# Cross attention in a decoder layer: two chunks of heads pass each stage of the loop together

## What is computed

```python
# per batch (8): L = 256 tokens, D = 128, H = 16 heads of DH = 64
q = layernorm(x) @ Wq          # 256 x 1024
k, v = layernorm(ctx) @ Wkv    # 256 x 1024 each
p = softmax(q k^T * DH**-0.5)  # per head, 256 x 256
x = layernorm(x + (p v) @ Wo + bo)
```

## Time and profile before

| | us |
|---|---|
| median of 3 runs (lowest, highest) | 2374.88 (2374.52, 2377.05) |
| span of the profiled execution | 2376.2 |
| PE busy over the span | 2232.7 (94%) |
| DVE busy | 1862.1 (78%) |
| ACT busy | 1703.2 (72%) |
| POOL busy | 1649.6 (69%) |
| mean granted TensorE clock | 0.981 |

### The profile page before, as it was taken

The page is one execution under the profiler, slowest core; times in us unless marked ns, Lnnn a source line. Parts: engine busy times, 40 slices in busy tenths (PEclk is TensorE's granted clock), DMA queues, the critical chain, the costliest instruction groups (busy, mean ns, idle before and its releaser), DMA issues. The chain is left out here.

```text
span 2376.2 us, 69401 instructions
## 1 busy us (share of the span) xinstructions
PE 2232.7 (94%) x26001; PEld 1464.0 (62%) x26001; DVE 1862.1 (78%) x2680; ACT 1703.2 (72%) x3299; POOL 1649.6 (69%) x1553
## 2 busy tenths in 40 slices
PE   5889779999799999999999999999999999999996
PEld 3555446666456666666666666666666666666664
DVE  4899957777678888888888888888888888887884
ACT  5889734544377787787787777787777777777774
POOL 4777832323478778778787787787787787787782
PEclk8999989999899999999999999999999999999997
DMA  2312210000022222222222222222222222222221
GB/s 76 111 59 68 69 51 2 1 1 1 20 63 67 56 76 66 61 71 66 64 68 66 68 65 66 72 61 67 74 58 67 78 54 67 78 53 67 78 53 52
DMA packets 103196, 140.36 MB, mean 59 GB/s; under 512 B 63072, under 2 KB 64096, under 8 KB 102752
## 3 DMA queue, kind: packets, MB, share of 16 engines
q1 hardware_dynamic: 103136, 139.57, 21.7%
HBM read 56.39 MB, written 1.31 MB: 24 GB/s over the span
## 5 line engine op out<-in xcount | busy, mean ns | idle before, releaser
L1799 PE MATMUL f_psA<-f_W,f_xT 128*128 (+1 forms) x1152 | 602.0, 632 | 20.7 <-DVE f_m L1607 12.5
L1607 DVE TENSOR_TENSOR f_m<-f_psA,f_tab 128x1024 f32<-128x1024 f32 x384 | 461.5, 1222 | 120.2 <-ACT f_sq L1468 106.1
L1357 POOL TENSOR_TENSOR f_Pr<-f_Pr,f_rden 128x384 f32<-128x384 f32 x384 | 311.5, 832 | 236.6 <-DVE f_rden L1586 236.6
L1385 POOL TENSOR_TENSOR f_qkr<-f_qkr,f_rn 128x1024 f32<-128x1024 f32 x192 | 361.5, 1904 | 0.2 <-POOL f_rn L1393 0.2
L1799 PEld LDWEIGHTS f_psA<-f_W,f_xT 128*128 128x128 f32 x1152 | 188.9, 190 | 164.5 <-issue 113.4
L1468 ACT ACTIVATE f_sq<-f_psA 128x512 f32<-128x512 f32 x384 | 228.2, 594 | 78.8 <-PE f_psA L1799 76.0
L1770 PEld LDWEIGHTS f_psO<-f_PT,f_V 96*64 96x64 f32 x6144 | 203.5, 138 | 96.4 <-issue 88.5
L1375 POOL TENSOR_TENSOR f_qkr<-f_m 128x512 f32<-128x512 f32 x192 | 244.2, 1272 | 9.1 <-DVE f_m L1607 9.1
L1376 POOL TENSOR_TENSOR f_qkr<-f_m 128x512 f32<-128x512 f32 x192 | 244.2, 1272 | 0.0
L1770 PE MATMUL f_psO<-f_PT,f_V 96*64 96x64 f32 x6144 | 231.9, 227 | 1.6 <-ACT f_PT L1443 1.5
L794 POOL TENSOR_TENSOR x_Es<-x_E 128x512 f32<-128x512 f32 x64 | 81.1, 1267 | 206.1 <-DVE x_E L899 206.1
(11 more groups left out here) (167 smaller groups left out, 4873.5 us busy)
## 6 DMA issues: line engine op xcount, KB each, us to landing
f_V<-f_Vt SPq DMA_DIRECT2D x96, 384.0 KB, 4.2
f_V<-f_Vt SPq DMA_DIRECT2D x96, 256.0 KB, 3.5
f_W<-in_f_W SPq DMA_DIRECT2D x48, 344.0 KB, 3.2
m_Cb<-m_BC_rows SPq DMA_DIRECT2D x64, 256.0 KB, 3.2
f_W<-in_f_W SPq DMA_DIRECT2D x48, 296.5 KB, 4.2
f_V<-f_Vt SPq DMA_DIRECT2D x48, 128.0 KB, 5.3
f_xsA<-xall SPq DMA_DIRECT2D x97, 32.0 KB
f_xsA<-xall SPq DMA_DIRECT2D x97, 31.8 KB
```

What stands on the lines that cost most here:

```text
L1357: pool.tensor_tensor(pv, pv, rv.unsqueeze(3).broadcast_to([P, 2, 2, KEYS]), ALU.mult).then_inc(Pr_ready[g][j], 1)
L1385: pool.tensor_tensor(qv, qv, rv.unsqueeze(3).broadcast_to([P, 2, GH, DH]), ALU.mult).then_inc(qkr_ready[g], 1)
L1607: dve.tensor_tensor(m12[:, j, :, half].rearrange("p m (h d) -> p m h d", d=DH), psA[n % 2][:, :].rearrange("p (h d) -> p h d", d=DH).unsqu ...
L1799: pe.matmul(psA[n % 2][:, :], xT[:, t, :], weights(i, W_QKV + n * 512, 512), start=True, stop=True).then_inc(A_full[n_fill], 1)
```

## The change

The loops go over pairs of chunks (g = 0, 2, 4, ...). Each engine's queue has both chunks of a pair at every stage. The whole output projection of the batch before is done in the pair c = 2, and so are its residual and moments. E has four buffers instead of two (ES = 4). In `scores` the key tile is the outer loop and the head the inner one, and there is one wait for both heads.

```diff
--- before.py
+++ after.py
@@ -691,6 +691,7 @@
     R = 2 * TPB
     LOADS = 16 * 7
     CHUNKS = B * NC
+    ES = 4
     LO, HI = float(np.exp(-11.0)), float(np.exp(11.0))
 
     with ExitStack() as ctx:
@@ -713,7 +714,7 @@
         ctxT = sb("x_ctxT", [P, 2, L])
         V1 = sb("x_V1", [P, 2, TPB, H, DH])
         qk = sb("x_qk", [P, 2, 2, L])
-        E = sb("x_E", [P, 2, 2, TPB, L])
+        E = sb("x_E", [P, ES, 2, TPB, L])
         Es = sb("x_Es", [P, 2, 2, L])
         rden = sb("x_rden", [P, 2, L])
         OT = sb("x_OT", [P, 2, NC, L])
@@ -747,19 +748,19 @@
 
         block = ctx.enter_context(nc.Block())
 
-        fills = [(0, "cat"), (0, "qk0")]
-        for g in range(CHUNKS + 1):
+        fills = [(0, "cat"), (0, "qk0"), (0, "qk1")]
+        for g in range(0, CHUNKS + 1, 2):
             b, c = divmod(g, NC)
-            if g + 1 < CHUNKS:
-                fills.append(((g + 1) // NC, f"qk{(g + 1) % NC}"))
             if g == 0:
                 fills += [(0, f"v{n}") for n in range(4)]
-            if c == 1 and b >= 1:
+            if c == 2 and b >= 1:
                 fills.append((b - 1, "wo"))
-            if c == 3 and b + 1 < B:
+            if g + 2 < CHUNKS:
+                fills += [((g + 2) // NC, f"qk{(g + 2) % NC}"), ((g + 3) // NC, f"qk{(g + 3) % NC}")]
+            if c == 2 and b + 1 < B:
                 fills.append((b + 1, "cat"))
             if c >= 4 and b + 1 < B:
-                fills.append((b + 1, f"v{c - 4}"))
+                fills += [(b + 1, f"v{c - 4}"), (b + 1, f"v{c - 3}")]
         fills.append((B - 1, "wo"))
         place = {f: (k % 2, k // 2) for k, f in enumerate(fills)}
 
@@ -791,7 +792,7 @@
                 if g >= 2:
 
                     pool.wait_ge(O_full, g - 1)
-                pool.tensor_tensor(Es[:, g % 2, :, :], E[:, g % 2, :, 0, :], E[:, g % 2, :, 1, :], ALU.add).then_inc(Es_ready, 1)
+                pool.tensor_tensor(Es[:, g % 2, :, :], E[:, g % ES, :, 0, :], E[:, g % ES, :, 1, :], ALU.add).then_inc(Es_ready, 1)
 
             def add_bias(b):
                 if b >= 1:
@@ -839,10 +840,10 @@
             def exponentials(g):
                 for j in range(2):
                     act.wait_ge(S_full, 2 * g + j + 1)
-                    if j == 0 and g >= 2:
-
-                        act.wait_ge(O_full, g - 1)
-                    act.activation(E[:, g % 2, j, :, :], psS[(2 * g + j) % 4][:, :, :], ACT.Exp, scale=DH ** -0.5).then_inc(E_exp, 1)
+                    if j == 0 and g >= ES:
+
+                        act.wait_ge(O_full, g - ES + 1)
+                    act.activation(E[:, g % ES, j, :, :], psS[(2 * g + j) % 4][:, :, :], ACT.Exp, scale=DH ** -0.5).then_inc(E_exp, 1)
 
             def copy_qk(g):
                 ps, free = wait_fill(act, g // NC, f"qk{g % NC}")
@@ -854,23 +855,27 @@
             deviation(0)
             scale_transposed(0)
             copy_qk(0)
-            for g in range(CHUNKS + 1):
+            copy_qk(1)
+            for g in range(0, CHUNKS + 1, 2):
                 b, c = divmod(g, NC)
-                if g + 1 < CHUNKS:
-                    copy_qk(g + 1)
                 if g < CHUNKS:
                     exponentials(g)
+                    exponentials(g + 1)
                 if g == 0:
                     for n in range(4):
                         evacuate_v(0, n)
-                if c == 1 and b + 1 < B:
+                if g + 2 < CHUNKS:
+                    copy_qk(g + 2)
+                    copy_qk(g + 3)
+                if c == 0 and b + 1 < B:
                     deviation(b + 1)
-                if c == 3 and b >= 1:
+                if c == 4 and b >= 1:
                     deviation2(b - 1)
-                if c == 3 and b + 1 < B:
+                if c == 2 and b + 1 < B:
                     scale_transposed(b + 1)
                 if c >= 4 and b + 1 < B:
                     evacuate_v(b + 1, c - 4)
+                    evacuate_v(b + 1, c - 3)
             deviation2(B - 1)
 
         @block.vector
@@ -896,7 +901,7 @@
             def clip(g):
                 for j in range(2):
                     dve.wait_ge(E_exp, 2 * g + j + 1)
-                    dve.tensor_scalar(E[:, g % 2, j, :, :], E[:, g % 2, j, :, :], LO, HI, ALU.max, ALU.min).then_inc(E_ready, 1)
+                    dve.tensor_scalar(E[:, g % ES, j, :, :], E[:, g % ES, j, :, :], LO, HI, ALU.max, ALU.min).then_inc(E_ready, 1)
 
             def normalise(g):
                 dve.wait_ge(O_full, g + 1)
@@ -920,21 +925,24 @@
 
             statistics(0)
             hats(0)
-            for g in range(CHUNKS + 1):
+            for g in range(0, CHUNKS + 1, 2):
                 b, c = divmod(g, NC)
-                if c == 2 and b >= 1:
-                    residual(b - 1)
                 if g < CHUNKS:
                     clip(g)
-                if g >= 1:
+                if c == 2 and b + 1 < B:
+                    hats(b + 1)
+                if g >= 2:
+                    normalise(g - 2)
+                if g < CHUNKS:
+                    clip(g + 1)
+                if g >= 2:
                     normalise(g - 1)
                 if c == 0 and b + 1 < B:
                     statistics(b + 1)
-                if c == 2 and b + 1 < B:
-                    hats(b + 1)
                 if c == 2 and b >= 1:
+                    residual(b - 1)
                     moments2(b - 1)
-                if c == 4 and b >= 1:
+                if c == 6 and b >= 1:
                     finish(b - 1)
             residual(B - 1)
             moments2(B - 1)
@@ -974,14 +982,14 @@
 
             def scores(g):
                 wait_evacuated(pe, g // NC, f"qk{g % NC}")
-                for j in range(2):
-                    h = 2 * g + j
-                    if h >= 4:
-                        pe.wait_ge(E_exp, h - 3)
-                    r = slice(j * DH, (j + 1) * DH)
-                    for kt in range(TPB):
-                        ins = pe.matmul(psS[h % 4][:, kt, :], qk[r, g % 2, 1, kt * P:(kt + 1) * P], qk[r, g % 2, 0, :], start=True, stop=True)
-                    ins.then_inc(S_full, 1)
+                if g >= 2:
+                    pe.wait_ge(E_exp, 2 * g - 2)
+                for kt in range(TPB):
+                    for j in range(2):
+                        r = slice(j * DH, (j + 1) * DH)
+                        ins = pe.matmul(psS[(2 * g + j) % 4][:, kt, :], qk[r, g % 2, 1, kt * P:(kt + 1) * P], qk[r, g % 2, 0, :], start=True, stop=True)
+                        if kt == TPB - 1:
+                            ins.then_inc(S_full, 1)
 
             def times_v(g):
                 b, c = divmod(g, NC)
@@ -994,7 +1002,7 @@
                     pe.wait_ge(O_free, g - 1)
                 for kt in range(TPB):
                     for j in range(2):
-                        pe.matmul(psO[g % 2][j * DH:(j + 1) * DH, 0, :], V1[:, b % 2, kt, 2 * c + j, :], E[:, g % 2, j, kt, :],
+                        pe.matmul(psO[g % 2][j * DH:(j + 1) * DH, 0, :], V1[:, b % 2, kt, 2 * c + j, :], E[:, g % ES, j, kt, :],
                                   start=(kt == 0), stop=(kt == TPB - 1), skip_group_check=True)
                 pe.wait_ge(Es_ready, g + 2)
                 for j in range(2):
@@ -1015,25 +1023,29 @@
 
             transpose_rows(0)
             project(0)
-            for g in range(CHUNKS + 1):
+            project(1)
+            for g in range(0, CHUNKS + 1, 2):
                 b, c = divmod(g, NC)
-                if g + 1 < CHUNKS:
-                    project(g + 1)
-                if c == 2 and b >= 1:
-                    out_projection(b - 1, 1)
                 if g < CHUNKS:
                     scores(g)
+                    scores(g + 1)
                 if g == 0:
                     for n in range(4):
                         project_v(0, n)
-                if g >= 1:
+                if g >= 2:
+                    times_v(g - 2)
                     times_v(g - 1)
-                if c == 1 and b >= 1:
+                if c == 2 and b >= 1:
                     out_projection(b - 1, 0)
-                if c == 3 and b + 1 < B:
+                    out_projection(b - 1, 1)
+                if g + 2 < CHUNKS:
+                    project(g + 2)
+                    project(g + 3)
+                if c == 2 and b + 1 < B:
                     transpose_rows(b + 1)
                 if c >= 4 and b + 1 < B:
                     project_v(b + 1, c - 4)
+                    project_v(b + 1, c - 3)
             out_projection(B - 1, 0)
             out_projection(B - 1, 1)
```

## The result

| | before | after |
|---|---|---|
| median of the runs, us | 2376.12 (5 runs) | 2388.03 (5 runs) |
| ratio, 95% interval | | 1.0047 [1.0034, 1.0059] |
| span of the profiled execution | 2376.2 | 2386.6 |
| end of the stage on TensorE, from the span's start | 622.06 | 633.80 |

One of the five runs of before took 3500.09 us, far from the other four (2374.52 to 2377.05, median 2375.50), and is left out of the ratio.

A forecast was written before the change was run, and what follows sets the result against it. The prediction took the stage, cross attention, as bound by TensorE. Its terms -17.9 + 14.4 + 1.4 + 2.5 = +0.4, plus 6.8 for the clock, gave +7.2 us: 2382 us, range 2369 to 2388.

The forecast's parts named there:

- Borders, -17.9: TensorE's three switches of tiling mode per chunk, then only per pair: 32 x 0.56 = 17.9 us less.
- V's late loads, +1.4: V projections waiting for the bank that copy_qk empties: up to 0.1 at both V's of 14 pairs, 1.4 us more.
- The pause, +14.4: TensorE waiting at project(g+3) of c = 2 for VectorE's residual: 2.4 us in six batches, 14.4 us more.
- Then the hats 1.02: Link of VectorE's path to the residual: the hats for the next batch take 1.02 us (twice 0.51).
- cost nothing: GpSimd's sums of tiles, 1.3 us a chunk, have a whole pair's time and so add nothing.
- Order of the heads, costed at nothing: In the scores, alternating the two heads gains nothing, because the pairs already run side by side.
- Rival (c): In the scores, heads overlap only when alternated: 0.86 us a chunk, 55 us won, 2327; chance 0.01.
- The clock, +6.8: TensorE's clock falls after four of the six new pauses, 1.7 us each: 6.8 us more, bounds 0 and 10.2.
- rival (a): No new pause lowers TensorE's clock: +0.4 us in all, 2375.3; chance 0.22, with cases of one or two falls.
- The final pause loses its 1.7 before and after alike: Clock loss after TensorE's pause at the stage's end: 1.7 us in both kernels, so no difference.
- The end, +2.5: Last pair of the stage: TensorE's waits become 1.3, 1.5 and 3.3 us, 2.5 more, bounds 1.5 to 3.5.
- Rival (b): At residual(b-1) VectorE comes early enough: pause 1.2 us, 2368, or no pause, 2361; chance 0.15.

The follow-up runs named there:

- experiment 10: Experiment 1's kernel with TensorE's scores and V products of the two chunks in turn again; 2375.43 us, ratio 0.9996.
- experiment 9: The changed kernel with the edits of experiment 1, experiment 2 and experiment 8, start flag set once per bank so nothing is left out; 2361.36 us, ratio 0.9940.
- experiment 2: The changed kernel, but GpSimd's sum of tiles in c = 2 waits until VectorE has written the hats; 2382.57 us, ratio 1.0030.
- experiment 4: The changed kernel with the heads in turn inside a chunk's scores and a wait for each head; 2389.33 us, ratio 1.0060.
- experiment 5: The kernel before, with only the scores' heads alternating and one wait for both; 2376.22 us, ratio 1.0000.
- Experiment 3: The changed kernel with project(g+2) of c = 2 computed four times over in batches 1 to 6; 2384.20 us, ratio 1.0034.
- experiment 8: Experiment 1's kernel with twelve of the last sixteen matmuls ahead of the final wait; one tile lacks six chunks; 2363.77 us, ratio 0.9950.
- experiment 1: The changed kernel with VectorE's residual directly behind the first normalisation of the pair c = 2 instead of behind both; 2368.36 us, ratio 0.9964.
- experiment 7: The changed kernel with ScalarE's Ln and Exp for the next batch behind c = 2's exponentials, and the hats behind the residual; 2369.46 us, ratio 0.9971.
- experiment 6: Experiment 1's kernel with two E buffers instead of four; 2380.30 us, ratio 1.0018.

## Why the prediction was right, and where a term was mis-sized

Direction, place and mechanism were right: slower, because of one wait per batch at project(g+3) of c = 2 that VectorE's residual releases, and because TensorE's clock falls after some of these. The number was 4.7 us too small, mostly by the pause (5.3 short). It would have been further off without two things that I had not foreseen: the clock held after the last pause in after and not in before (1.6), and it fell after three pauses where I took four.

- **Borders, -17.9:** right in the plain pairs, 0.56 each by the profile, and experiment 10 gives two of the borders their 0.35. The pair c = 2 saves only about 0.4 instead of 0.56 (10.71 in experiment 9; before, 7.55 for c = 2 and 3 and 3.58 for the output projection, 11.13), which the forecast doesn't have: 0.9 us in six batches, and with it most of the way from the 12.2 forecast for them to the 11.1 measured. Batch 0 is right once the shift of one chunk's V is taken out.
- **V's late loads, +1.4:** right. The two pairs with V projections take 8.46 and 8.41; without the loads they would take 8.88 - 0.56 = 8.32 (two chunks of 4.44 before). 0.23 a batch, 1.6 in seven.
- **The pause, +14.4: the step that failed is "Then the hats 1.02".** It measured 1.98, because GpSimd's sum of tiles, which used to run elsewhere, now runs beside one hat. That is 0.96 x 6 = 5.8, and experiment 2 gives 0.95 back for a wait on GpSimd alone. Every other link of VectorE's path was within about 0.1 (together they took 0.15 less), TensorE's path within 0.05. I had written that GpSimd's sums "cost nothing" since they had a pair's time. That was true of their own duration, and said nothing of whom they stand next to.
- **Order of the heads, costed at nothing:** not quite. It is 0.1 of the 0.56 a pair (experiments 4 and 5): the rows of before could show that the heads run side by side inside a chunk, but not what happens where two chunks' scores meet. So of the 0.56 about 0.1 is the order's and not a border's. Rival (c), 0.86 a chunk, is out by both.
- **The clock, +6.8:** measured 6.0 in the six batches, from three falls instead of four, one of them nearly twice as dear as the others: near the forecast in part by luck. Experiment 3 shows it is the pause that costs it: with the pause filled it never fell. So rival (a) had a real chance; a profile in which the clock held would have read some 6 less. "The final pause loses its 1.7 before and after alike" was wrong for the two profiles: before lost 1.6 there and after nothing.
- **The end, +2.5:** the three waits measured 2.5, and experiment 8 shows how to take the last of them away.
- **Rival (b), VectorE early enough:** false for the change as made. But the state that it describes is what experiments 1, 7 and 9 make on purpose: 2368, 2369 and 2361. Its prices, 2368 and 2361, look right and are not: 2368 was meant for a pause of 1.2, and experiment 1 reads it with 0.33; 2361, 14.0 below before, was meant for no pause with the end as it is, and experiment 9 without the 3.5 that experiment 8's edit gave is about 11 below. (The chances of (b) and (c) add up to 0.16, not 0.15.)

## What to carry to other kernels

When stages are taken two at a time, write out the queue of each waiting engine from one instant to the release, and look for a short instruction that now stands behind long ones: moving it (here a residual of 0.4 us) was worth 20 us. Sum the durations of such a path only after asking what will run beside each of them: the same instruction on VectorE took 0.34 alone and 1.30 when it started behind a sum on GpSimd. And where a pause cannot be removed, work that is thrown away can be cheaper than the clock that the pause costs.

## What the runs showed of the hardware that I had not expected

- **A VectorE tensor_scalar from SBUF to SBUF stood still for a whole GpSimd instruction** (1.295 instead of 0.34, ending 0.08 after it). A clip in the first pair of the stage shows the same; of the 1.84 for two clips here the second took 1.35, where 0.43 is usual.

```profile
333.94 1.84 DVE L904 TENSOR_SCALAR x_E<-x_E 128x512 f32<-128x512 f32 x2
335.70 0.47 DVE L47 BATCH_NORM_STATS2 x_stats<-xall 128x6 f32<-128x128 f32 x2
```

```profile
334.03 1.46 POOL L795 TENSOR_TENSOR x_Es<-x_E 128x512 f32<-128x512 f32 x1 [11.91 <-DVE x_E L904]
```

Not every instruction is held. The statistics, which also read and write SBUF, took the same 0.47 beside GpSimd's next sum (335.86 to 337.13) as in the earlier trace rows. VectorE's reciprocal, which reads PSUM, was not touched either: the one at 559.35, with GpSimd's sum beside it from 559.75 to 561.02, took 1.76, and the one at 569.56, with none beside it, 1.75.
- **Equal pauses, unequal clocks.** The pauses of after are the same to 0.01 us, and the work around them too; yet the clock fell after three of six, and cost 2.8 us once and 1.6 and 1.5 the other times. At 3.0 it fell after two of six (experiment 4), at 2.17 after three of six (experiment 2), and after none of the six of 1.49 (experiment 6). How long the pause is did not decide alone whether the clock fell; what did, no run here shows.
- **Two chunks' scores join without a seam only if the heads alternate:** sixteen passes from row to row 1.93 in alternation and 2.03 in turn, while the eight of one chunk alone made no difference.
